# One load of function tables, one order of P times V products and one place of the softmax outputs in the second attention layer of a two-layer network

## The reference

```
def _L1_attn_ref(X, Wq, bq, Wk, bk, Wv, bv, Wo, bo):
    HEADS, HEAD_DIM = 16, 16
    Q = X @ Wq + bq; K = X @ Wk + bk; V = X @ Wv + bv      # split into 16 heads of 16
    scores = jnp.einsum('bhqd,bhkd->bhqk', q, k) / np.sqrt(HEAD_DIM)
    attn = jax.nn.softmax(scores, axis=-1)
    out = jnp.einsum('bhqk,bhkd->bhqd', attn, v)
    return out @ Wo + bo

def _L1_ffn_ref(x, W0, bias0, W1, bias1):                  # 256 -> 1024 -> 256, float16 between
    D = jax.nn.gelu(x @ W0.T + bias0, approximate=False)
    return D @ W1.T + bias1

x = x + s * _silu(g)
```

## Time and profile before

| | us |
|---|---|
| median of 3 runs | 1032.8 |
| lowest and highest | 1026.98, 1033.57 |
| the profiled execution, its own time | 1032.8 |
| its span, first to last instruction | 1031.0 |
| busy in the span: TensorE | 901.3 (87%) |
| VectorE | 664.4 (64%) |
| ScalarE | 498.0 (48%) |
| GpSimd | 281.2 (27%) |
| start of the first Exp (L744) of layer 1, batch by batch | 260.09, 495.54, 730.82, 966.19 |

### The profile page before, as it was taken

How to read it: one execution, slowest core, us unless ns; L and a number is a source line. 1 busy time by engine, 2 the same in 40 slices (tenths; PEclk the granted TensorE clock), 3 DMA queues, 4 the chain that set the end, 5 groups by cost and what they waited for, 6 DMA issues and landing times.

```text
span 1031.0 us, 14430 instructions
## 1 busy us (share of the span) xinstructions
PE 901.3 (87%) x5184; PEld 559.7 (54%) x5184; DVE 664.4 (64%) x1656; ACT 498.0 (48%) x987; POOL 281.2 (27%) x216
## 2 busy tenths in 40 slices
PE   3737697979988999979988999979988999979996
PEld 1425365845434677845434767855434667855533
DVE  3986567656856566655956666655956666644963
ACT  4455465323673666223573766313563666314463
POOL 0663656100001577100000667200000657300000
PEclk9877699989998999989998999989998999989998
DMA  7310001118001010018101110008200100007300
GB/s 222 93 36 11 16 21 38 50 53 214 2 2 46 28 56 17 1 39 207 22 2 36 38 47 26 2 3 223 42 2 25 47 27 1 1 1 189 79 2 21
DMA packets 45751, 51.24 MB, mean 50 GB/s; under 512 B 6000, under 2 KB 35440, under 8 KB 45680
## 3 DMA queue, kind: packets, MB, share of 16 engines
q1 hardware_dynamic: 42976, 47.47, 17.1%
q10 hardware_dynamic: 2384, 1.79, 0.6%
q0 software_dynamic: 320, 1.05, 0.3%
HBM read 37.44 MB, written 12.58 MB: 49 GB/s over the span
## 4 chain that ended last, share of the span: by engine, by line
PE 66%; DVE 15%; ACT 8%; DMA 3%; issue 3%; SPq 2%; POOL 1%; POOLq 0%; DVEq 0%; ACTq 0%
PE bank L792 12%; PE bank L834 6%; PE bank L1033 6%; PE bank L881 5%; PE bank L909 5%; PE bank L893 5%; PE bank L1018 5%; PE bank L1045 4%; PE bank L990 3%; DVE mx L1372 3%; ACT region L744 3%; PE bank L1023 3%; DVE w1T L1122 2%; PE bank L872 2%; PE bank L846 2%
## 5 line engine op out<-in xcount | busy, mean ns | idle before, releaser
L519 POOL TENSOR_TENSOR region<-region 128x512 f32<-128x512 f32 x80 | 109.6, 1370 | 463.8 <-DVE region L1217 459.1
L1372 DVE TENSOR_REDUCE mx<-bank 128x1 f32<-128x512 f32 x256 | 162.9, 682 | 53.9 <-PE bank L990 52.8
L744 ACT ACTIVATE region<-bank 128x512 f32<-128x512 f32 x256 | 139.0, 595 | 71.8 <-PE bank L1023 66.4
L792 PE MATMUL bank<-xnT,wrope 128*128 128x512 f32 x320 | 149.6, 611 | 8.1 <-ACT xnT L623 8.1
L656 ACT ACTIVATE region<-region,nb 128x224 f32<-128x224 f32 (+1 forms) x256 | 97.6, 451 | 108.7 <-DVE nb L1226 108.3
L834 PE MATMUL bank<-V,region 128*128 128x224 f32 x384 | 91.2, 384 | 28.3 <-DVE nb L1226 21.7
L1018 PE MATMUL bank<-Qp,Kp 64*128 64x512 f32 x256 | 88.8, 473 | 18.6 <-ACT region L744 18.4
L515 POOL TENSOR_TENSOR region<-region,sin_sb 128x512 f32<-128x512 f32 x60 | 78.5, 1308 | 85.5 <-ACT region L636 85.5
L792 PEld LDWEIGHTS bank<-xnT,wrope 128*128 128x128 f32 x320 | 62.1, 198 | 70.0 <-issue 60.5
L834 PEld LDWEIGHTS bank<-V,region 128*128 128x128 f32 x384 | 73.4, 201 | 40.6 <-DVE nb L1226 23.9
L1018 PEld LDWEIGHTS bank<-Qp,Kp 64*128 64x128 f32 x256 | 35.4, 183 | 96.4 <-ACT region L744 79.4
(11 more groups left out here) (131 smaller groups left out, 1484.1 us busy)
## 6 DMA issues: line engine op xcount, KB each, us to landing
wrope<-in_wrope SPq DMA_DIRECT2D x80, 128.0 KB, 2.1
scratch<-region SPq DMA_DIRECT2D x32, 256.0 KB, 3.7
Qp<-scratch SPq DMA_DIRECT2D x64, 128.0 KB, 3.6
Kp<-scratch SPq DMA_DIRECT2D x64, 128.0 KB, 3.7
X<-in_x SPq DMA_DIRECT2D x4, 512.0 KB, 4.0
scratch<-region SPq DMA_DIRECT2D x16, 128.0 KB, 3.7
out<-X SPq DMA_DIRECT2D x16, 128.0 KB, 1.7
wpT<-in_wgu SPq DMA_DIRECT2D x3, 512.0 KB, 12.3
```

Of the source, the lines that this page charges most:

```text
L519: nc.gpsimd.tensor_tensor(dst, dst, sw[:, r % 2, :], ALU.add)\
L744: nc.scalar.activation(P1[:, n % 8, :], t_ring[n % 3][:, :], ACT.Exp, scale=SCALE1)\
L792: mm = nc.tensor.matmul(misc(name)[:, 0:width], lhs(c), xnT[:, c, :], start=(c == 0), stop=(c == DC - 1))
L1372: nc.vector.tensor_reduce(mx1[:, g % 2, column:column + 1], s_ring[m % 3][:, :], AX.X, ALU.max)\
```

## The change

On ScalarE, the tile `warm` and its Exp are removed, and the fourth `half_tanh1` stands before the group loop with the three others instead of behind Exp 3. On TensorE, `attend1(g, 3)` stands at the end of its own group, behind attend1(g, 2), instead of behind the first block of the next group. On VectorE, the fourth gate stands behind maximum 31 instead of 35, and `outputs1(g - 2)`, called in the numbering of the scores ahead, stands behind the maximum with i = 13 of its group instead of behind i = 15 and `negate_max`.

```diff
-        warm = sb("warm", [P, 1])
...
-                nc.scalar.activation(warm[:, :], ones1[:, :], ACT.Exp)
                 half_tanh1(0)
                 max_high(0)
-                for t in range(1, TT - 1):
+                for t in range(1, TT):
                     half_tanh1(t)
...
-                        if n == 3:
-                            half_tanh1(TT - 1)
                         if i == 5 and g + 1 < NG:
                             max_high(g + 1)
...
-                        if k or g:
-                            attend1(g if k else g - 1, (k - 1) % TT)
-                attend1(NG - 1, TT - 1)
+                        if k:
+                            attend1(g, k - 1)
+                    attend1(g, TT - 1)
...
-                FFN_ROWS, GATES = (12, 17, 22, 27), (16, 21, 26, 35)
+                FFN_ROWS, GATES = (12, 17, 22, 27), (16, 21, 26, 31)
...
                     if i == 15:
                         negate_max(g)
-                    if i == 15 and g >= 2:
-                        outputs1(b, g - 2)
...
                     if m in GATES:
                         t = GATES.index(m)
                         gate_of(b, 1, t, e16[:, t, 0:DIM])
+                    if i == 13 and g >= 2:
+                        outputs1(b, g - 2)
```

## The result

| | before, us | after, us |
|---|---|---|
| median | 1031.9 | 1069.87 |
| lowest and highest | 1026.98, 1033.57 | 1066.21, 1077.95 |
| span of the profiled execution | 1031.0 | 1066.6 |
| mean granted clock of TensorE in it | 0.943 | 0.933 |

The medians are of four executions of each kernel. The ratio is 1.0416, 95% interval 1.0369 to 1.0462; it compares means and uses 29 of the 31 executions of the changed kernel on record (1066.21 to 1081.14, median 1073.8), without the two slow ones of 1084.03 and 1091.47. The forecast was 1056 with a range to 1067; the direction was right, the amount too small by 14 us, and the time just outside the range.

The account below looks back on a forecast made before the run. TensorE bounds the kernel, busy two thirds of the span, with little slack on any engine in a block. Profiled 1032.8 us plus waits of 20.0 gave 1052.8, plus 3.4 for the clock 1056 us; range 1045 to 1067.

Parts of the forecast that it names:

- the rhythm of a block: Layer 1 attention: a regular block takes 3.29 us; ScalarE has 1.02 and VectorE 0.78 of slack in it.
- Edit 1: ScalarE, loop entry: warm Exp removed, fourth half_tanh1 ahead of all Exp; first Exp 2.23 late, costing 2.04 us a batch.
- the upper end: ScalarE: Gelu table serves Tanh, so the 1.28 us load stands on the path before the first Exp; taken at 0.8.
- Edits 2 and 3: TensorE's attend1(g, 3) and VectorE's outputs1 moved: 0.20 at group 3, 1.04 at group 1, 1.72 at group 2, a batch.
- The sum of the waits: Waits at the entry and the starts of groups 1, 2 and 3: 5.00 us a batch, 20.0 in four.
- The clock: TensorE idle 2.5 us before its fourth turned score; half of four half-clock falls at 1.7 counted, 3.4 us.
- Clock falls fully in all four batches: Rival: TensorE loses 3.4 us in each batch behind the entry's idle time, 13.6 in all; 1066 us, chance 0.17.
- the dearer switch: Rival: ScalarE's table switch costs DRAIN besides its load, and TensorE's clock falls each time; 1072 us, chance 0.03.
- The load hidden: Rival: the first Tanh takes the table load in ScalarE's rest; entry +0.7, batch +3.7, 1048 us, chance 0.20.
- The not slower case: Rival: outputs1 fits VectorE's rest, load hidden, if negate_max ends by 3.4 us after block start; 1031 to 1033, chance 0.08.

Follow-up runs that it names:

- edit 2 alone: Kernel before with only attend1(g, 3) moved to the end of its own group, outputs1 still behind negate_max: 1039.65 us, ratio 1.0072.
- the filled version of the changed kernel: Changed kernel plus unused 512-column matmuls in TensorE's new idle times: before the fourth turned score and at groups 1 and 2; 1051.26 us, ratio 1.0207.
- the last: Changed kernel with unused matmuls in its three new idle times and in the two that both kernels have: 1041.73 us, ratio 1.0115.
- the narrow matmuls: Changed kernel with unused matmuls 16 columns wide instead of 512 in TensorE's new idle times, same places and waits: 1073.44 us, ratio 1.0394.
- edits 2 and 3: Kernel before with only the new order of attend1 and place of outputs1, ScalarE's part as before, nothing filled: 1056.31 us, ratio 1.0252.

## Why the prediction failed, point by point

**What bounds the kernel, the rhythm of a block.** Right. The block in the earlier trace rows carried the terms of the waits.

**Edit 1.** Right in place and nearly in size: 2.34 a batch for 2.04, by the loops with the idle time filled. The second block already starts 2.23 late there, the figure forecast for the first Exp; the forecast let the rest of the entry take 0.19 of it back, and it added 0.1 instead. The choice of the upper end (the load in front of the first Exp) was right, and the load took 1.28, with no DRAIN: it ran from 260.89, 0.01 behind the Tanh, and Exp started 0.02 behind it. This speaks against the 2.66 us of the Trainium skill (ScalarE: Activation LUTs, What ACT_TABLE_LOAD costs) for this chip and this place, as the earlier trace rows did. One supporting sentence was wrong: "The load does not wait for the Exp's input". It did no harm, since the input was already there when the Tanh ended, but the kernel with the warm Exp removed alone shows that this load does wait.

**Edits 2 and 3.** Right: 2.98 for 2.96 a batch, and edit 2 alone 1.30. By the starts of the blocks, with the idle times filled, group 1 costs 1.04 (forecast 1.04), group 2 1.59 (1.72) and group 3 the last 0.34 (0.20): in the filled version of the changed kernel group 3 starts 1.02 late and its first two blocks take 5.44 (303.38 to 308.82) in place of 6.12. That the sum agrees to 0.02 is luck, since the two small misses cancel.

**The sum of the waits.** 5.3 a batch for 5.0, 21.1 in the loops for 20.0.

**The clock.** This is the step that failed, a term of the sum that was far too small. The prediction put the clock at 3.4 us, half of four falls at 1.7, and at 13.6 as the bound from above, "3.4 in each batch". The runs put 18.6 us in the loops. Some 4 us came back outside them, where I had expected nothing to move: 1031.0 + 21.1 + 18.6 - 4.1 is the span of 1066.6. Three things were wrong in this step. It looked only at the entry's idle time of 2.5 us and not at those that its own working had just put at the starts of groups 1 and 2, "about 2 us in all at each of two places" (measured 1.36 and 1.87); of 51 us at 1.2 GHz in the loops, 20.4 (3.4, 3.4, 6.8 and 6.8) lie behind the entry and 30.6 behind the borders of groups. It took an idle time's length as what matters, by two single rows, where edit 2 alone shows a fall behind 0.21, 0.22 and 0.89 us in a row. And it capped the falls at one a batch, where batch 3 has four. The price that it set, half of a stretch, erred the other way: the loops paid 0.36 us for each us.

**The rivals.** "Clock falls fully in all four batches", 1066, was right in kind, its cap too low. In number the dearer switch, 1072, came nearest, but by luck: its own cause, a switch that costs more than its load, is not in the trace (0.01 and 0.02 us beside the load, above). The load hidden, 1048, did not come: the trace has no load at any Tanh behind a Gelu, so here the Gelu's table serves Tanh. The list of the Trainium skill (ScalarE: Activation LUTs, Table sets: the hidden batching unit) names tanh in the sets of exp and of sigmoid and not in that of gelu; this trace does not bear that out. The not slower case fell by its own condition: VectorE's negation ended at T+5.15 at the start of group 1 (281.40 less 276.25), forecast T+5.17.

**The range.** It reached to 1067 by this cap. With the three new idle times of a batch in it, none to all of them with a fall at 1.7, it would have run from 1053 to 1052.8 + 12 * 1.7 = 1073 and held the result. That is said with the result known, and 1.7 is not a bound on a fall: batches 2 and 3 have stretches of 6.8 us.

## What to carry to other kernels

List every idle time that a change gives TensorE, the short ones and those in clusters too, and price each as a possible fall of the clock behind it; here that was nearly as much as the waits themselves (18.6 and 21.1 us). Where TensorE must wait, matmuls without use in a free bank that end before the release kept the clock up in most loops (all four of the first filled version, three of four in the last), and they tell the price of the clock apart from that of the wait. The warm Exp, which only brings a table forward, was worth its 0.2 us in both kernels: about 1% of the time each.

## What the runs showed of the hardware

A stretch at 1.2 GHz in a loop lasted 3.4 or 6.8 us mostly, once 10.2 (the narrow matmuls) and once 13.7 (edits 2 and 3), though no idle time before it was longer than 2.5 us and some were only 0.2 to 0.5. The stretches don't come at the same places in each batch: in the changed kernel the idle time of 1.87 us at group 2 brought one in batches 2 and 3 and none in batches 0 and 1 of the same execution, and with edits 2 and 3 alone it brought one in all four. The executions of the changed kernel vary with it: one took 1066.21 us at a mean clock of 0.934, another 1077.95 at 0.917. What decides between the places is open; no run here tries it.

A table load on ScalarE waited for the semaphore of the Exp behind it when two waits stood in front of that Exp (2.94 us of rest unused), and did not wait in front of the Gelu, which has one: there it ran 2.76 us ahead of the data. Whether the number of waits is the cause was not tried.
